# A vision-transformer tower: the exponentials of the scores are written in SBUF over the differences, three buffers deep, and a score bank is released when the differences are taken

## What is computed

```python
h = _L0_tok_ref(x, Wp, bp)                              # 16 x 36 x 192
h = _layernorm(h + _L0_attn_ref(h, w_qkv, w_out, b_out))
h = _layernorm(h + _L0_ffn_ref(h, ...))
# inside both layers, for each head or expert:
score = einsum(q, k) * scale                            # 36 x 36 of each image (band or causal mask)
weights = softmax(score)                                # the part that the change touches
out = einsum(weights, v)
```

## Time and profile before

| | |
|---|---|
| three unprofiled executions | 114.75, 114.96, 116.04 us; median 114.96 |
| the profiled execution | 115.59 us, of which the span of the instructions is 113.8 |
| PE busy | 104.5 us (92%) |
| PEld busy | 93.7 us (82%) |
| DVE busy | 76.7 us (67%) |
| ACT busy | 72.2 us (63%) |
| POOL busy | 21.5 us (19%) |

### The profile page before, as it was taken

How to read it: one execution, slowest core, us unless ns; L and a number is a source line. 1 busy time by engine, 2 the same in 40 slices (tenths; PEclk the granted TensorE clock), 3 DMA queues, 4 the chain that set the end, 5 groups by cost and what they waited for, 6 DMA issues and landing times.

```text
span 113.8 us, 3528 instructions
## 1 busy us (share of the span) xinstructions
PE 104.5 (92%) x1381; PEld 93.7 (82%) x1381; DVE 76.7 (67%) x240; ACT 72.2 (63%) x200; POOL 21.5 (19%) x34
## 2 busy tenths in 40 slices
PE   6999999999999999999999999999969878978940
PEld 4699899997799989799988998999958777876920
DVE  0565909276935787249585978887767779988661
ACT  4577784588898775946954378762366468539260
POOL 7003624554156500000493000000000000000000
PEclk9999999999999999999999999999999999999998
DMA  3999999200000000000000000000000000000202
GB/s 75 333 347 402 411 418 424 84 0 6 3 0 6 3 0 6 0 6 0 0 0 6 0 0 6 6 0 0 0 3 6 3 0 6 0 0 0 64 19 78
DMA packets 4124, 7.73 MB, mean 68 GB/s; under 512 B 1293, under 2 KB 2445, under 8 KB 3981
## 3 DMA queue, kind: packets, MB, share of 16 engines
q1 hardware_dynamic: 3740, 7.24, 17.6%
q10 hardware_dynamic: 368, 0.28, 0.7%
HBM read 7.08 MB, written 0.44 MB: 66 GB/s over the span
## 4 chain that ended last, share of the span: by engine, by line
PE 65%; DVE 16%; DMA 5%; issue 5%; ACT 3%; SPq 3%; DVEq 0%
PE proj L933 11%; PE score L1014 8%; PE outp L1059 7%; DMA x_f<-x_t 5%; PE outp L897 5%; PE proj L918 4%; PE trans L1038 4%; PE proj L925 3%; PE proj L919 3%; PE proj L922 3%; PE proj L926 3%; DVE wqk_f L759 2%; DVE ln_st L744 2%; ACT ln_ln L566 2%; SPq L375 1%
## 5 line engine op out<-in xcount | busy, mean ns | idle before, releaser
L545 ACT ACTIVATE pt_t<-trans,image_t 108x216 f32<-108x216 f32 (+1 forms) x42 | 14.6, 425 | 3.7 <-PE trans L1038 3.3
L1014 PE MATMUL score<-k_t,q_t 64*36 64x37 f32 (+1 forms) x416 | 10.5, 196 | 0.0
L1014 PEld LDWEIGHTS score<-k_t,q_t 64*36 64x36 f32 x416 | 9.0, 111 | 1.6 <-issue 1.0
L529 ACT ACTIVATE score<-d_t 128x296 f32<-128x296 f32 (+2 forms) x16 | 6.6, 413 | 5.8 <-DVE d_t L708 5.8
L705 DVE TENSOR_REDUCE mx_t<-score 128x8 f32<-128x296 f32 (+2 forms) x16 | 7.1, 444 | 4.5 <-PE score L1022 4.2
L718 DVE TENSOR_REDUCE sm_t<-score 128x8 f32<-128x288 f32 (+1 forms) x16 | 7.0, 438 | 4.2 <-ACT score L529 4.2
L566 ACT ACTIVATE ln_ln<-ln_mv,const 108x1 f32<-108x1 f32 (+1 forms) x12 | 3.6, 297 | 8.6 <-DVE ln_mv L747 8.6
L657 DVE TENSOR_TENSOR x_lo<-x_f,x_hi 128x288 fp32r<-128x288 f32 x12 | 6.3, 534 | 4.0 <-ACT x_hi L461 4.0
L505 ACT ACTIVATE q_t<-proj 128x288 f32<-128x288 f32 x12 | 5.0, 417 | 6.2 <-PE proj L926 5.9
L933 PE MATMUL proj<-wv_hi,h_hi 128*108 128x384 f32 (+1 forms) x24 | 8.2, 343 | 0.0
L418 POOL TENSOR_TENSOR wqk_lo<-wqk_f,wqk_hi 128x256 fp32r<-128x256 f32 x6 | 4.5, 756 | 18.1 <-ACT wqk_hi L465 18.1
(11 more groups left out here) (208 smaller groups left out, 341.5 us busy)
## 6 DMA issues: line engine op xcount, KB each, us to landing
ffn_f<-f_w SPq DMA_DIRECT2D x1, 1088.0 KB, 12.2
wqk_f<-w_qk SPq DMA_DIRECT2D x2, 512.0 KB, 8.2
x_f<-x_t SPq DMA_DIRECT2D x2, 432.0 KB, 6.5
wv_f<-w_v SPq DMA_DIRECT2D x1, 768.0 KB, 7.4
wo_f<-w_out SPq DMA_DIRECT2D x1, 768.0 KB, 9.9
x_f<-x_t SPq DMA_DIRECT2D x2, 288.0 KB, 4.8
tw_f<-tok_w SPq DMA_DIRECT2D x2, 256.0 KB, 4.6
wqk_f<-w_qk SPq DMA_DIRECT2D x2, 256.0 KB, 5.9
```

Source lines behind the costliest of these rows:

```text
L545: nc.scalar.activation(pt_t[:, n % 2, 0:tiles, :, i], trans[0:ROWS, 0:tiles, :, 0:TOK], ACT.Copy, scale=image_t[:, i:i + 1]).then_inc(spli ...
L1014: ins = nc.tensor.matmul(s[64 * h:64 * h + TOK, im, 0:width], q, k_t[rows, n % QK_RING, im, 0:width], start=(kind == "attn" and im == 0), ...
```

## The change

The differences get three buffers in SBUF. The exponential is written over the differences that it reads, not into the score bank, and the sums and the scaling on DVE read it there. The bank is free when the differences are taken, so all waits of PE for a score bank go by `shifted` where they went by `normed`. DVE, before it writes differences into a buffer, waits for `normed` of the entry three back (its own work), where it waited for `exped` of the entry two back. No instruction is added, removed or moved on any engine: the order of each engine is the same row by row, and only operands and waits differ.

```diff
+D_RING = 3
-        d_t = sb("d_t", [128, 2, GI, KEYS])
+        d_t = sb("d_t", [128, D_RING, GI, KEYS])
...
             def exp_scores(n):
-                s, slots, width = by_key(n)
+                _, slots, width = by_key(n)
                 act.wait_ge(shifted, n + 1)
-                nc.scalar.activation(s[:, :, 0:width], d_t[:, n % 2, 0:slots, 0:width], ACT.Exp, scale=SCALE).then_inc(exped, 1)
+                d = d_t[:, n % D_RING, 0:slots, 0:width]
+                nc.scalar.activation(d, d, ACT.Exp, scale=SCALE).then_inc(exped, 1)
...
-                if n >= 2:
-                    dve.wait_ge(exped, n - 1)
-                nc.vector.tensor_tensor(d_t[:, n % 2, 0:slots, 0:width], s[:, :, 0:width],
+                if n >= D_RING:
+                    dve.wait_ge(normed, n - D_RING + 1)
+                nc.vector.tensor_tensor(d_t[:, n % D_RING, 0:slots, 0:width], s[:, :, 0:width],
...
             def normalise(n):
-                e, slots, width = by_key(n)
+                _, slots, width = by_key(n)
+                e = d_t[:, n % D_RING, 0:slots]
...
                 if n >= 2:
-                    pe.wait_ge(normed, n - 1)
+                    pe.wait_ge(shifted, n - 1)
...
                 if in_score((g, t)):
-                    pe.wait_ge(normed, ENTRY_OF[("attn", g, PAIRS - 2 + t)] + 1)
+                    pe.wait_ge(shifted, ENTRY_OF[("attn", g, PAIRS - 2 + t)] + 1)
...
-                        pe.wait_ge(normed, len(ENTRIES))
+                        pe.wait_ge(shifted, len(ENTRIES))
```

## The result

| | median | executions |
|---|---|---|
| before | 115.25 us | 114.75 to 116.04 (4) |
| changed | 116.72 us | 116.11 to 116.88 (4) |
| ratio | 1.0102 | 95% interval 1.0069 to 1.0135 |

The change costs 1.0%, or 1.2 us (0.8 to 1.6); the two medians lie 1.47 us apart, which is inside that interval. I had forecast 0.6 us of loss: the direction was right, the loss was twice as large as forecast, and the median lies above my range.

The account below looks back on a forecast made before the run. PE was taken to bound the kernel from 17 to 80 us, then a chain between PE, DVE and ACT. The terms 0 + 0.02 + 0.61 = +0.63 us on the median 114.96 gave 115.6 us, range 114.6 to 116.3.

Parts of the forecast that it names:

- What bounds the kernel: PE busy 62.62 of 63.00 us from 17 to 80 us; any wait there goes to the end at full price.
- Part 1: PE's waits for the score banks: `s 2`, `s 10` and `s 11` have no idle time ahead, so gain 0.
- Part 2: Instructions that change place, on the chain after 80 us: DVE's taken as 0, one ACT exponential +0.02 us.
- The estimate of -0.35 us: Last stretch: the skill's access overheads for six DVE instructions and one exponential; left out of the sum.
- Part 3: DVE instructions with two SBUF inputs wait for POOL's subtraction; entry 3's `t 3` starts late, PE stands still 0.61 us.
- The high end adds entry 2: DVE 0.19 us late at entry 2; `t 2` then loses nothing, slips by 0.2 us, or comes 1.0 us late.
- I take 0.61: Size chosen for the DVE-beside-POOL loss, from entry 3 alone: 0.61 us, low end 0 or 0.17.
- the first of my three cases: Entry 2: POOL's start slips with ACT's, DVE's scaling goes first, no loss.
- PE is late by the larger of the two: Losses at entries 2 and 3 don't add; the end of entry 3's scaling stays at 39.3.
- POOL holds up more than entry 3: Rival: loss also at entry 2, or `pv 3` behind late entry 3; 116.0 to 116.5 us, chance 0.2.
- No lock on these forms: Rival: broadcast or 8-column DVE instructions don't wait for POOL; 115.0 us, up to 115.15, chance 0.2.
- Shorter access to SBUF: Rival: six DVE instructions in the last stretch get faster; about 115.3 us with entry 3's loss, 114.6 without; chance 0.1.

Follow-up runs that it names:

- e1: The changed kernel, but PE waits for a score bank by `normed` as before the change; exponentials stay in SBUF. 1.0095 of before.
- e2: The change applied to entries 4 to 15 only; entries 0 to 3 keep exponentials in the PSUM bank and the old wait. 0.9984 of before.
- e4: The kernel before, with the exponentials of entries 0, 1 and 2 alone in SBUF. 1.0069 of before.
- e9: The changed kernel with ACT's copies of entry 3's q and k ahead of entry 2's exponential. 1.0069 of before.
- e3: The kernel before, with the exponentials of entry 3 alone in SBUF. 1.0039 of before.
- e5: The changed kernel with POOL's long subtraction for the output weights cut in six pieces. 1.0063 of before.
- e10: The changed kernel with the edits of e5 and e9 together. 1.0044 of before.
- e6: The changed kernel with POOL's long subtraction for the output weights replaced by one memset of the same tile. 1.0047 of before.
- e8: The changed kernel with POOL's long subtraction replaced by the memset done three times, PE waiting for the third. One execution, 115.78 us.
- e7: The changed kernel with PE's old waits and the softmax's sums, reciprocals and shares in spare PSUM columns of the score bank. 1.0007 of before.

## Why the prediction came out as it did

**What bounds the kernel: right.** PE without slack up to 80 us meant that each stall went to the end: 1.28 us of steps in the profile, 1.2 by the ratio. There was one idle time that I had overlooked, 0.26 us at 59.53, where PE waits for DVE's `wqk_f` (L761). It gave nothing back: it is 0.25 in the changed kernel.

**Part 1, the waits are worth 0: right.** e1 shows it: the old waits with the exponentials in SBUF give the changed kernel's time as closely as intervals of 0.3 to 0.4% can tell, and its `t 3` and `t 4` to the hundredth.

**Part 2, +0.02 us: right.** The scaling stayed at 458 ns, the row sums at 447 (452 before), the exponential grew by 29 ns where I had 21, and the last stretch by 0.02 us. The estimate of -0.35 us that I worked out from figures of the Trainium skill (Perfetto Trace Analysis, Optimizing Scalar/DVE Operations) didn't come true: the six DVE instructions of the last stretch read SBUF in the changed kernel and in e2, and from `t 8` to entry 14's transposes it is 33.57 us in both, where it was 33.55. (The ratio of e2 by itself, from 0.9957, couldn't exclude a gain of 0.35 us.)

**Part 3, DVE beside POOL, 0.61 us: the mechanism right, the term at half its size.** I took 0.61 and it measured 1.28. The part for entry 3 came out at 0.61, as worked out (11.61 - 10.44 - 0.56), with L723 at 1.45 us. What failed is the step "The high end adds entry 2", and with it "I take 0.61". I let the POOL instruction at 28.02 hold up only entry 1's scaling, and put DVE 0.19 us late for entry 2. In fact the short L723 was caught in entry 0 and in entry 1 already, by 0.57 and 0.51 us. Before, L720 stood at 24.60 in entry 0, and POOL had an instruction that ended some hundredths of a microsecond earlier and the next that began some hundredths later; I didn't look at that gap, and in entry 1 I looked at the scaling alone. An instruction of 0.23 us is caught as well as one of 0.46, and stands, like it, until POOL's is over. By entry 2's differences DVE was (29.51 - 28.01) - (29.27 - 28.42) = 0.65 us late.

Then I followed that delay to `t 2` only. There it costs nothing by itself: POOL's start slipped with ACT's and DVE had the way at 31.72, the first of my three cases. But entry 2's exponential stands on ACT ahead of the copies that free the banks of `qk 4`, and that cost 0.56 us two steps ahead of `t 2`. I had asked who waits on PE and DVE, and not who is queued on ACT. e4 shows this term by itself, e9 that nothing else held `qk 4`. I also took the two losses for alternatives ("PE is late by the larger of the two"). They add, since the L723 of entry 3 had moved with its own work (37.29 - 28.01 = 9.28, before 37.12 - 28.42 = 8.70) and so had POOL's long subtraction, which starts when ACT's copy of the output weights is done, and ACT was late with PE: 35.21 - 28.01 = 7.20, before 6.64.

The remaining 0.11 us between `t 3` and `t 4` appear wherever `t 3` is late behind DVE (e1, e3, e5, e9, e10 and the changed kernel), and not in e4, e6 or e8. I had named `pv 3` as having a tenth or two to spare, and the matmuls of `pv 2` and `pv 3` take 1.31 us in the changed kernel and took 1.22; ACT's copies of entry 3 (`sp 3`), which `pv 3` waits for, end at 42.19, and the first matmul of `pv 3` starts 0.14 us behind their end, in e3 likewise; before, it started 0.36 behind. They stand on ACT behind entry 4's exponential, and that behind the late DVE, which is the same pattern as at `qk 4`; no experiment moved them, so this cause is argued and not shown.

**The rivals.** "POOL holds up more than entry 3" was the case that came true: its loss of 1.0 to 1.5 us holds the measured 1.2, at another place than I had put it. I gave it 0.2. The time of 116.72 us lies above even its 116.5 because the kernel before came out at 115.25 us and not at the 114.96 from which I had counted: of the 1.1 us between forecast and median, 0.3 are the start and the rest is the loss. "No lock on these forms" fell: a broadcast factor and eight columns behave as full operands. "Shorter access to SBUF" fell with the steps from `t 8` on, in the changed kernel and in e2.

## What to carry to other kernels

Before an operand moves from PSUM to SBUF, count the SBUF inputs of each DVE instruction that reads it, the short ones too; one that comes to have two must not meet a POOL instruction that reads SBUF, or it stands until that is over. Moving the small operand (here eight sums a row) to PSUM (e7), or leaving the entries that meet POOL as they were (e2), cost nothing that could be measured. And a delay on one engine is followed along every queue that its result stands in: here the price was paid by copies that stood behind the late exponential and had no data in common with it.

## What the runs showed of the hardware

- With two SBUF inputs, an eight-column DVE instruction of 0.23 us stood for up to 1.22 us behind one POOL subtraction; the end of its row lies 0.02 to 0.03 us behind POOL's. It got in between two of POOL's queued pieces (e5). Beside a POOL memset it didn't stand (e8), nor with one input in PSUM (e7).
- Either engine can be the one that waits: with both rows starting at once, POOL's subtraction took 1.06 and 1.05 us instead of 0.74 beside DVE's scaling (changed kernel, e4), and DVE's scaling took 1.05 instead of 0.46 when POOL's row began 0.01 us sooner (e1). But the short instruction of entry 0 waited though its row began 0.04 us ahead of POOL's (changed kernel), and that of entry 1 waited from a level start. Where two rows start within 0.04 us of each other, their starts don't say which of the two pays.
- DVE's row sums and scaling of 288 columns took 447 and 458 ns from SBUF, 452 and 457 from PSUM. ACT's exponential of 288 columns took 443 ns into SBUF and 414 into PSUM, that of 296 columns 454 and 428.
